# OMP sparse coding behind a convolution: two convolutions cut in halves between the updates, two reconstructions moved to the round's end

## What is computed

```python
x = x + conv3x3(gn(x), ternary(w)) + b + sigmoid(gate) * (conv3x3(gn(x), ternary(w_child)) + b_child)
# second step: every 4 x 4 patch of gn(x) with its 32 channels is a signal of 512 values
D = dictionary / norm(dictionary)                 # [512, 256]
G = D.T @ D + 1e-5 * eye(256)
h_bar = (D.T @ X).T ; h = h_bar                   # X: [512, 4096 patches]
for k in range(1, 6):                             # 5 greedy steps
    index = argmax(abs(h * not_yet_chosen))
    x_stack = solve(G on the chosen atoms, h_bar on them)
    h = h_bar - x_stack @ G[chosen]
x = x + (D @ coeffs) as patches
```

## Time and profile before

| | us |
|---|---|
| runs (3), median | 556.13 |
| lowest, highest | 554.5, 557.31 |
| the profiled execution | 555.17 |
| its span, first to last instruction | 553.3 |
| DVE busy | 458.7 (83%) |
| PE busy | 409.0 (74%) |
| ACT busy | 309.3 (56%) |
| mean granted TensorE clock | 0.891 |

### The profile page before, as it was taken

One profiled execution on the slowest core, in us unless ns is written; L12 is line 12 of the kernel. 1 busy time (PEld: TensorE's weight loads), 2 busy tenths in 40 slices (PEclk: granted clock), 3 DMA queues, 4 the chain that ended last, 5 costly groups with the idle time before them and its releaser, 6 DMA issues.

```text
span 553.3 us, 7423 instructions
## 1 busy us (share of the span) xinstructions
PE 409.0 (74%) x1666; PEld 296.3 (54%) x1666; DVE 458.7 (83%) x2325; ACT 309.3 (56%) x682; POOL 149.8 (27%) x162
## 2 busy tenths in 40 slices
PE   0099885899666669889893979998839557788674
PEld 0032772355556556456682854567738435676453
DVE  4483657878898979969999899989998999799990
ACT  2544436586656467668687385976802443465133
POOL 3000035334200063522300464433003644330010
PEclk9999996989878688989997979999978866899598
DMA  5979212789400025997510277613101754124155
GB/s 101 173 104 170 60 39 68 126 131 156 91 0 2 0 81 115 201 175 115 127 26 1 63 168 150 134 57 78 39 0 30 176 130 100 52 67 96 39 113 115
DMA packets 110202, 50.71 MB, mean 92 GB/s; under 512 B 103632, under 2 KB 104144, under 8 KB 110160
## 3 DMA queue, kind: packets, MB, share of 16 engines
q1 hardware_dynamic: 102000, 26.13, 28.9%
q0 software_dynamic: 8160, 24.13, 18.9%
HBM read 34.24 MB, written 8.65 MB: 78 GB/s over the span
## 4 chain that ended last, share of the span: by engine, by line
PE 43%; DVE 31%; ACT 8%; issue 6%; SPq 6%; DMA 5%; DVEq 0%; ACTq 0%
PE h L387 30%; PE conv_ps L387 10%; DVE junk L992 8%; DVE coef L1113 4%; DVE top L922 3%; DMA xb<-in_x 3%; SPq L248 3%; DVE top_i L935 3%; DVE top_i L937 2%; ACT score L636 2%; PE back_ps L387 2%; ACT diag L645 2%; ACT xb L602 2%; SPq L255 2%; DVE coef L1109 1%
## 5 line engine op out<-in xcount | busy, mean ns | idle before, releaser
L359 POOL DMA_INDIRECT rows<-gram,idx_u x128 | 131.5, 1027 | 346.7 <-DVEq L979 317.2
L387 PE MATMUL h<-rows,diag 128*128 128x256 f32 x640 | 165.9, 420 | 49.8 <-ACT diag L645 47.6
L387 PEld LDWEIGHTS h<-rows,diag 128*128 128x128 f32 x640 | 133.0, 212 | 83.6 <-issue 60.0
L645 ACT ACTIVATE diag<-ident,dx 128x128 f32<-128x128 f32 x320 | 96.8, 387 | 40.6 <-DVEq L1094 37.5
L992 DVE SCALAR_TENSOR_TENSOR junk<-mask,rows 128x256 bf16<-128x256 bf16 x320 | 119.4, 421 | 0.0
L636 ACT ACTIVATE score<-h 128x512 f32<-128x512 f32 x80 | 47.3, 597 | 99.4 <-PE h L387 99.0
L922 DVE MAX8 top<-score 128x8 f32<-128x256 f32 x160 | 65.3, 422 | 33.9 <-ACT score L636 32.3
L387 PE MATMUL h<-d_sb,z 128*128 128x256 f32 x256 | 66.6, 424 | 3.5 <-DVEq L913 2.5
L387 PE MATMUL back_ps<-coef_t,d_t 128*128 128x256 f32 x224 | 58.3, 419 | 13.3 <-ACT coef_t L651 13.3
L387 PEld LDWEIGHTS h<-d_sb,z 128*128 128x128 f32 x256 | 63.2, 330 | 6.9 <-issue 3.2
L387 PE MATMUL conv_ps<-xa,w_taps 128*64 128x512 f32 x128 | 61.7, 604 | 1.4 <-ACT x L614 1.0
(11 more groups left out here) (152 smaller groups left out, 506.0 us busy)
## 6 DMA issues: line engine op xcount, KB each, us to landing
xa<-in_x SPq DMA_DIRECT2D x64, 128.0 KB, 5.4
out<-x SPq DMA_DIRECT2D x64, 128.0 KB, 2.9
x<-y POOLq DMA_DIRECT2D x14, 512.0 KB, 4.7
xb<-in_x SPq DMA_DIRECT2D x42, 128.0 KB, 4.2
rows<-gram,idx_u POOLq DMA_INDIRECT x128, 3.1
xb<-in_x SPq DMA_DIRECT2D x14, 120.0 KB, 5.2
rows<-in_x SPq DMA_DIRECT2D x6, 128.0 KB, 4.4
d_sb<-in_L_conv_dictionary SPq DMA_DIRECT2D x4, 128.0 KB, 4.0
```

Of the source, the lines that this page charges most:

```text
L359: pool.indirect_dma_start(out=rows[s][:, k, t, :], out_offset=None, in_=gram_dram[:, :], in_offset=bass.IndirectOffsetOnAxis(ap=idx_u[s][: ...
L387: return nc.tensor.matmul(dst, lhs, rhs, start=start, stop=stop, skip_group_check=skip)
L645: last = nc.scalar.activation(diag[s][:, t, j, :], ident[:, :], ACT.Copy, scale=dx[s][:, k, t, j:j + 1])
```

## The change

- PE: `conv` is split into `conv_half`. Image 2: half 0 before update(r,0,2), half 1 behind it. Image 3: half 0 behind that, half 1 behind update(r,1,2). `y_sums` moves from ahead of update(r,0,3) to behind it. The transposes and reconstructions of images 2 and 3 of round b move from between the updates to the round's end, behind correlate(f, 0).
- ACT: evictions follow in halves, the squares one by one between them; square_sum(f,3) stands behind diags(r,0,3); copy and eviction of the moved reconstructions stand at the round's end, with the statistics of images 0 and 1 of the next front between them.
- POOL: the adds of images 2 and 3 of a round move behind gather(r,0,0) of the second round after it. Before, that of image 2 stood behind gather(r,1,3) one round earlier.
- SP: the stores of images 2 and 3 move to the top of the second round after theirs.
- DVE: nothing.

```diff
@@ SP
             def body(r, front, more, behind):
+                if r > 1:
+                    store(r - 2, 2)
+                    store(r - 2, 3)
                 if behind:
                     store(r - 1, 0)
                 if front:
                     loads_ahead(r + 1, more)
                 if behind:
-                    for m in range(1, IMG_R):
-                        store(r - 1, m)
+                    store(r - 1, 1)
...
@@ POOL
-            added_after = {(0, 1): 0, (1, 1): 1, (3, 1): 2}
+            added_after = {(0, 1): 0, (1, 1): 1}
...
                         if r > 1 and (k, s) == (0, 0):
+                            add_back(IMG_R * (r - 1) - 2)
                             add_back(IMG_R * (r - 1) - 1)
...
@@ PE, body
                 update(r, 1, 1)
                 if front:
-                    conv(f, 2)
+                    conv_half(f, 2, 0)
                 update(r, 0, 2)
                 if front:
-                    conv(f, 3)
+                    conv_half(f, 2, 1)
+                    conv_half(f, 3, 0)
+                update(r, 1, 2)
+                if front:
+                    conv_half(f, 3, 1)
+                update(r, 0, 3)
+                if front:
+                    y_sums(f)
+                update(r, 1, 3)
+                if front:
+                    correlate(f, 0)
                 if behind:
-                    coef_transposes(b, 2)
-                update(r, 1, 2)
-                if behind:
-                    reconstruct(b, 2)
-                if front:
-                    y_sums(f)
-                update(r, 0, 3)
-                if behind:
-                    coef_transposes(b, 3)
-                    reconstruct(b, 3)
-                update(r, 1, 3)
-                if front:
-                    correlate(f, 0)
+                    for m in range(2, IMG_R):
+                        coef_transposes(b, m)
+                        reconstruct(b, m)
@@ ACT, body
                 if front and behind:
-                    for m in range(IMG_R):
-                        x_statistics(f, m)
+                    x_statistics(f, 2)
+                    x_statistics(f, 3)
...
                 diags(r, 0, 2)
                 if front:
-                    out_conv(f, 2)
+                    out_half(f, 2, 0)
                 scores(r, 0, 3)
                 if front:
+                    out_half(f, 2, 1)
                     square_sum(f, 0)
+                diags(r, 1, 2)
+                if front:
+                    out_half(f, 3, 0)
                     square_sum(f, 1)
-                diags(r, 1, 2)
-                if front:
-                    out_conv(f, 3)
-                if behind:
-                    copy_coef(b, 2)
                 scores(r, 1, 3)
                 if front:
+                    out_half(f, 3, 1)
                     square_sum(f, 2)
+                diags(r, 0, 3)
+                if front:
                     square_sum(f, 3)
-                diags(r, 0, 3)
-                if behind:
-                    out_back(b, 2)
+                scores(r, 0, 4)
                 if front:
                     root(y_var, y_root, 1, f)
-                scores(r, 0, 4)
-                if behind:
-                    copy_coef(b, 3)
                 diags(r, 1, 3)
...
                     scores(f, 0, 0)
+                if behind:
+                    for m in range(2, IMG_R):
+                        copy_coef(b, m)
+                        if f + 1 < ROUNDS:
+                            x_statistics(f + 1, m - 2)
+                        out_back(b, m)
+                elif front:
+                    x_statistics(f + 1, 0)
+                    x_statistics(f + 1, 1)
```

More of the change, by code:

```diff
@@ L319, in _ @@
             body(ROUNDS - 1, False, False, True)
+            for m in range(2, IMG_R):
+                store(ROUNDS - 2, m)
             for m in range(IMG_R):
@@ L378, in _ @@
                             add_back(IMG_R * (r - 1) + added_after[k, s])
-            add_back(IMG_R * (ROUNDS - 1) - 1)
+            for n in range(IMG_R * (ROUNDS - 1) - 2, IMG_R * (ROUNDS - 1)):
+                add_back(n)
             for n in range(IMG_R * (ROUNDS - 1), BY_DMA):
@@ L422, in y_sums, with conv_half @@
                    True, True).then_inc(y_stats_ps, 1)
-            def conv(f, m):
-                n = IMG_R * f + m
-                hold(pe, x_normed, n + 1)
-                if isinstance(n, int) and n == 0:
-                    pe.wait_ge(x_normed_act, 1)
-                hold(pe, w_mid_ready, f + 1)
-                for b in range(2):
-                    if not (isinstance(f, int) and f == 0 and m == 0):
-                        hold(pe, x1_done, 2 * n - 1 + b)
-                    for i, kx in enumerate((0, 2, 1)):
-                        wk = w_mid[:, m, :] if kx == 1 else w_taps[:, kx, :]
-                        rows_ = slice(b * GR // 2, (b + 1) * GR // 2)
-                        for half, src in enumerate((xa[:, m], b_part(f, m))):
-                            part = slice(half * P // 2, (half + 1) * P // 2)
-                            last = mm(conv_ps[part, b, :], wk[:, part], src[:, rows_, kx:kx + W], i == 0, i == 2, True)
-                    last.then_inc(conv_done, 1)
+            def conv_half(f, m, b):
+                n = IMG_R * f + m
+                if b == 0:
+                    pe.wait_ge(x_normed, n + 1)
+                    if n == 0:
+                        pe.wait_ge(x_normed_act, 1)
+                    pe.wait_ge(w_mid_ready, f + 1)
+                if n > 0:
+                    pe.wait_ge(x1_done, 2 * n - 1 + b)
+                for i, kx in enumerate((0, 2, 1)):
+                    wk = w_mid[:, m, :] if kx == 1 else w_taps[:, kx, :]
+                    rows_ = slice(b * GR // 2, (b + 1) * GR // 2)
+                    for half, src in enumerate((xa[:, m], b_part(f, m))):
+                        part = slice(half * P // 2, (half + 1) * P // 2)
+                        last = mm(conv_ps[part, b, :], wk[:, part], src[:, rows_, kx:kx + W], i == 0, i == 2, True)
+                last.then_inc(conv_done, 1)
+            def conv(f, m):
+                for b in range(2):
+                    conv_half(f, m, b)
             def correlate(f, s):
@@ L606, in image_of, with out_half @@
                 return t[:, n % KEPT, :]
+            def out_half(f, m, b):
+                n = IMG_R * f + m
+                act.wait_ge(conv_done, 2 * n + 1 + b)
+                if b == 0 and n >= KEPT:
+                    act.wait_ge(place_stored[n - KEPT], 16 * PATCH)
+                nc.scalar.activation(image_of(x1, n)[:, b * HALF:(b + 1) * HALF], conv_ps[:, b, :], ACT.Identity,
+                                     bias=gn[:, 0, 10, m:m + 1], accum_out=sum_1[:, b, m:m + 1]).then_inc(x1_done, 1)
             def out_conv(f, m):
-                n = IMG_R * f + m
                 for b in range(2):
-                    hold(act, conv_done, 2 * n + 1 + b)
-                    if b == 0 and n >= KEPT:
-                        act.wait_ge(place_stored[n - KEPT], 16 * PATCH)
-                    nc.scalar.activation(image_of(x1, n)[:, b * HALF:(b + 1) * HALF], conv_ps[:, b, :], ACT.Identity,
-                                         bias=gn[:, 0, 10, m:m + 1], accum_out=sum_1[:, b, m:m + 1]).then_inc(x1_done, 1)
+                    out_half(f, m, b)
             def square_sum(f, m):
@@ L764, in body @@
                     norm_y(f, 1)
-                if behind:
-                    out_back(b, 3)
                 scores(r, 1, 4)
```

3 lines of the change are left out of this document (1 added, 2 removed).

## The result

| | before | after |
|---|---|---|
| median of the runs, us | 555.94 (4 runs) | 589.69 (4 runs) |
| lowest, highest | 554.5, 557.31 | 588.06, 591.66 |
| ratio after to before, 95% interval | | 1.0609 [1.0563, 1.0655] |
| span of the profiled execution | 553.3 | 588.9 |
| mean granted TensorE clock | 0.891 | 0.882 |

The change makes the kernel 6.1% slower. The forecast was 592.8 us, with +37.6 us of span; measured were 589.7 us and +35.6.

A forecast was written before the change was run, and what follows sets the result against it. The prediction took the kernel to be bound by a VectorE stream with holes, its order fixed. Round 0 6.0, round 1 9.3, round 2 14.2, round 3 5.0 and tail 3.1 added 37.6 to 555.2: 592.8 us, range 572 to 602.

The forecast's parts named there:

- The moved sums: VectorE's variance of y waits for sums behind update(0,3): +6.0 us in round 0, +7.7 each in rounds 1 and 2.
- What R(3) hid: Without image 3's reconstruction the TensorE idles ahead of update(1,3): +1.6 us each in rounds 1 and 2, round 0 nothing more.
- Halves between the updates: Half convolutions around update(0,2) gain nothing; idle time costs the clock: +1.7 us in round 2, 0 in rounds 0 and 1.
- The turns: Starts of rounds 2 and 3, where work waits for the later add of image 2: +3.2 and +2.7 us.
- the add of image 2: Now behind gather(r,0,0) on GpSimd; the eviction into y[0] waits for it: +3.2 us in round 2, +2.7 in round 3.
- T, R at the round's end: Transposes and reconstructions of images 2 and 3 fill TensorE's idle 9.37 us; sums of x come 1.0 us late, hidden.
- Round 3 and the tail: Low clock in update(0,3) and update(1,3), +2.3 us; a longer queue to the transposes of image 14, +3.1 us.
- The clock holds: Rival: the 3 us holes stay at 2.4 GHz and reconstructing at the round's end helps: 578.6 us, chance 0.18.
- Only the stall: Rival: only the wait for the sums costs; the add is early enough or hidden, clock holds: 572.7 us, chance 0.10.
- Worse: Rival: adds and gathers share the DMA queue, rows or stores late, 3 to 5 us in rounds 2, 3: 602, chance 0.08.
- Faster: Rival: the sums would not bind and the relieved middle gives back VectorE's waits for scores: 548 us, chance 0.03.

The follow-up runs named there:

- e3: Kernel before with only the sums of y moved behind update(0,3) on the TensorE: 566.22 us, 1.0207 of before.
- e4: Changed kernel with reconstructions of images 2 and 3, their adds, stores and statistics put back; halves and late sums stay: 574.94 us, 1.0381 of before.
- e6: Changed kernel plus matmuls whose result nobody reads, in the TensorE's holes around update(0,3) of rounds 0 to 2: 580.12 us, 1.0463 of before.
- e2: Changed kernel with the VectorE's variance of y moved later, to the search of (0,4), its parameters behind it: 576.46 us, 1.0426 of before.
- e8: Kernel before with norm_x of image 3 put behind diags(0,2) on the ScalarE: 551.41 us, 0.9951 of before.
- e1: Changed kernel with the sums of y again ahead of update(0,3), and image 3's square ahead of its diags: 579.60 us, 1.0465 of before.
- e7: Changed kernel with both adds of the round before ahead of gather(r,0,0) on GpSimd: 588.78 us, 1.0639 of before.
- e5: Kernel before with only the reconstructions of images 2 and 3 moved, with their transposes, adds, stores and statistics: 573.43 us, 1.0334 of before.
- e11: Kernel before plus unread matmuls at the turns and in the holes of round 0, ScalarE's order untouched: 544.67 us, 0.982 of before.
- e10: Kernel before with norm_x of image 3 behind diags(0,2) in rounds 1 and 2, plus unread matmuls at turns and in round 0: 550.53 us, 0.9888.

## Why the prediction was right

The mechanism was the one forecast, and the total came within 2 us of it, but partly by luck, because errors cancelled. Differences of the two traces at the VectorE's searches, taken apart by the terms of the sum:

| term | forecast | measured |
|---|---|---|
| round 0, up to update(0,3) | 0 (-0.8 to +0.9) | -1.1 |
| round 0, stall for the sums | 6.0 | 5.6 |
| round 0, behind it | 0 | -1.0 |
| round 1, halves around update(0,2) | 0 | 2.9 |
| round 1, stall | 7.7 | 7.5 |
| round 1, what R(3) hid | 1.6 | 1.7 |
| turn into round 2 | 3.2 | 3.6 |
| round 2, halves | 1.7 | 1.5 |
| round 2, stall | 7.7 | 7.4 |
| round 2, what R(3) hid | 1.6 | 1.1 |
| turn into round 3 | 2.7 | 2.6 |
| round 3, updates at k = 3 | 2.3 | 1.8 |
| tail | 3.1 | 2.1 |
| sum | 37.6 | 35.6 (35.7 by the rounded terms) |

**The moved sums.** Right in place, sign and size: 20.5 us of the 35.6. Of the 7.5 at the search (0,4) of round 1, 4.3 are the late sums alone (e3), 1.7 the halves ahead of the update (e4, 6.0), and the rest the clock (e6 wins 1.7 back there, and its wait is 6.03 instead of 7.71). e2 shows that the stall hangs on the reader's place. The row from which the slow update was priced held more idle time than the prediction read in it: in round 0 of before the sums ahead of update(0,3) had themselves waited.

```profile
140.68 0.39 PE L387 MATMUL conv_ps<-sum,same_channel 128*128 128x12 f32 x2 [2.76 <-ACT z L620]
```

So 2.76 and 1.48 us of idle time stood ahead of its 8.83 us, and in after one idle time of 3.18 gave 8.83 in round 1 as well, 8.64 and 8.74 in rounds 0 and 2. That the forecast met the first of these to a hundredth is luck: in e8 the same update of round 0 took 9.89 us, behind 2.76 and 2.35 of idle time.

**What R(3) hid.** Right in rounds 1 and 2 (in round 1 update(1,3) took 9.97 us after 10.27 of idle time); e6, which kept the clock there, ran it in 7.14 and won 1.7 at the next search. In round 0 the stall gave 1.0 us back, where I had put nothing.

**Halves between the updates: a term that the runs did not confirm.** I put 0 for round 1, since update(0,2) waited for a late load anyway, "so this hole only grows". It measured 2.9. The ScalarE's wait for the load was longer:

```profile
242.07 1.19 ACT L613 ACTIVATE xa<-xa,gn 128x960 f32<-128x960 f32 x1 [4.39 <-DMA xb<-in_x]
```

4.39 us against 2.60 in before, +1.8. This wait ended 10.3 us after the load's first issue, 8.3 in before. And the hole had grown to 6.25 us, behind which update(0,2) took 8.26 us instead of 7.11, +1.15, with a granted clock of 0.50 until 251 and 1.00 from 252.

I can't put this on the halves. The wait ended 10.2 us after the issue in e1, 8.7 in e2, 8.8 in e4, 8.6 in e6 and 9.1 in e7, all with the halves, and 9.2 in e3 and 9.4 in e5 without them. Where the load came sooner (e2, e4, e6, e7) the hole was 4.6 to 5.2 us and update(0,2) took 7.1 to 7.3 us, as in before; only after and e1 (5.87 us of idle time, 8.20) paid more. Against before, the search (0,3) loses 0.1 us in e2 and 0.5 to 0.9 in e4, e6 and e7, and 0.9 to 1.0 in e3 and e5, which have no halves. So the 0 for the halves stands within what such a load moves, and the 2.9 is a late landing with the clock loss behind it; what makes the load land late is open. In round 2, where the clock was the whole term, 1.7 was forecast and 1.5 measured (7.07 us after 2.55 of idle time).

**The turns.** In round 2 the total is right, 3.6 for 3.2, but I had put all of it on the add of image 2. By the searches, 0.7 stand at (1,0), 1.9 at (0,1) and 1.0 at (1,1). The 1.9 are the add's by a sum of rows: the eviction waited 3.13 us for it, and the normalization behind the eviction had waited 1.23 in before anyway. e7 does not confirm a price, as its R(3) ran slowly. The 1.0 at (1,1) stands behind a reconstruction that took 6.65 us after 2.94 of idle time (at 341.39). In round 3 the total (2.6 for 2.7) is right and the reason wrong. The 2.6 us are already there at the search (1,0), ahead of the add: R(3) at the round's end ran at the low clock.

```profile
442.20 5.41 PE L393 MATMUL back_ps<-coef_t,d_t 128*128 128x256 f32 x16 [0.69 <-ACT coef_t L666]
...
444.00:446.00 2.00, 2.00 (x7) 1.55 (x6) 2.00 (x7) 0.59 (x1) 0.00 (x0) 0.50 0.00 0
```

It took 5.41 us, for which I had put 3.72, with the correlation behind it late. The wait for the add (2.48 us on the ScalarE at 462.07) is then hidden, and e7 took it away for no gain. The step that failed is the 1.0 us that I gave to T, R at the round's end in a turn "with no clock to regain"; the clock can be lost there as well, and then the place costs 2.6. It is not lost every time: at the turn into round 2 of after R(3) ran in 3.72 us behind idle times of the same length (0.74, 1.26, 0.69), and in e6 and e7 it took 5.39 and 5.41.

```profile
315.33 3.72 PE L393 MATMUL back_ps<-coef_t,d_t 128*128 128x256 f32 x16 [0.69 <-ACT coef_t L666]
```

What decides between them stays open.

The adds landed in 4.5 to 9.1 us, median 5.1, against a forecast of about 5. The Trainium skill ("DMA: Bandwidth & Descriptors", Anatomy of one DMA) gives 3.2 us for 512 KB by its fit, an estimate. No add of these traces landed in less than 4.5 us.

**Round 3 and the tail.** update(0,3) cost 2.7 and update(1,3) 0.4, for 1.9 and 0.4, but 1.2 us had been given back ahead of them, in the middle of the round. 0.7 of it, at the search (1,2), is also in e3, e8 and e11, whose edits lie elsewhere, so the trace of before was late there; by what the rest was given back stays open. The tail was 3.1 by a queue of 29.4 us that I added up, and measured 2.1. The queue took 28.7 us, from the transposes at 543.17 to those of image 14 at 571.88.

**The rivals.** "The clock holds" (578.6) falls by the 8.83 and the 0.50 at 273. "Only the stall" falls by the turns and the clock. "Worse" (602), by which the rows for (1,0) would come late as well, falls by the turns, 3.6 and 2.6 us; the gathered rows landed in a median of 3.2 us, 3.1 in before. "Faster" needed update(0,3) to end before the VectorE's second pick; in round 1 it ended at 280.04, and the instruction behind that pick waited 7.71 us. That the moved reconstructions bring a gain of their own falls with e5. The Trainium skill ("TensorE: Matmul & The Clock Gate", HAM oscillation) ties the loss of the clock to idle gaps longer than the 3.18 us here; the trace disagrees. The Trainium skill ("TensorE: Matmul & The Clock Gate", A second HAM failure mode) tells of another kernel, which cycles through PSUM banks and loses the clock by idle times that are short but frequent. R(3) at 442.20 and e10's update(0,3) look like that, but R(3) at 315.33, with the same idle times and 3.72 us, does not, so these runs don't settle it.

## What to carry to other kernels

When a producer moves, look at where its reader stands in an in-order engine: two small matmuls, moved past one update, cost 4.3 us a round because their reader stood two picks into independent work, and moving the reader won 4.2 a round back. Work that looks like filler between bursts of matmuls may be what keeps TensorE's clock up; price its removal by the updates behind it at both clock levels, and add such work (even unread) where the engine idles and a chain follows. Where parts of a change share one hole or one clock loss, costs of the parts alone don't add: 20.5 and 19.0 gave 33.8. And before a difference of two traces is put on an edit, see whether it stands at a place that the edit reaches: one load moved several of these traces by 1 to 3 us.

## What the runs showed of the hardware

- Unread matmuls pay here: the fills of e11 took the mean clock from 0.891 to 0.939 and the time to 0.982 [0.9785, 0.9856] of before.
- The clock falls behind short idle times too: 1.47 us ahead of update(0,3) in e10 (with 0.60 a little earlier) went with 8.61 us; in e11, with the same 0.60 and the 1.47 filled, it took 7.07. An idle time as long does not always cost it: 1.54 us ahead of update(1,3) in e6 left 7.14. What the engine did before differs (40 matmuls in 8.88 us in e6; in e10 an idle time of 0.60 us and 6 small and unread matmuls).
- The same load of four parts of 120 KB from memory was waited for until 8.3 us after its first issue in before, 8.6 to 9.4 in six of the experiments (e2 to e7) and 10.2 to 10.3 in e1 and after. e2 differs from after only in the VectorE's order in steps 3 and 4 and had it 1.6 us sooner. That moves a stage by up to 2 us, and what follows the hole by the clock besides.
